# Two tiles' second-layer experts run in pairs behind the last dense pass, and the front stages get new spacings

## The reference

```python
h = W_E[tokens] * 16
h = h + time_and_channel_mix(layernorm(h))            # first layer's attention block
# first layer's experts ("dense"): 8 experts of 1024, mixed by a top-2 router, all computed
x = layernorm(h)
h = h + sum(w0[:, e] * (gelu(x @ W1[e] + b1[e]) @ W2[e] + b2[e]) for e in range(8))
# second layer's recurrence: k, v = x @ Wk, x @ Wr; running maximum, two scans, ratio
x = layernorm(h)
h = h + (sigmoid(r) * wkv(k, v)) @ Wo
# second layer's attention (16 heads of 16) and its four experts, top-2 of 4
x = layernorm(h)
xn = rms(x, n1_w); q, k, v = rms(heads(xn @ wq)), rms(heads(xn @ wk)), heads(xn @ wv)
x = x + zero_first_64(softmax(causal(q @ k.T)) @ v @ wo)
xf = rms(x, n2_w); w = top2(softmax(xf @ gate_w))
o0 = gelu(xf @ e0_up) @ e0_down
o1 = silu(xf @ e1_w1) * (xf @ e1_w2) @ e1_down
o2 = gelu(gelu(gelu(xf @ e2_l1) @ e2_l2) @ e2_l3) @ e2_l4
o3 = gelu(gelu(xf @ e3_down) @ e3_up) @ e3_out
h = h + x + zero_first_64(w[0]*o0 + w[1]*o1 + w[2]*o2 + w[3]*o3)
```

## Time and profile before

| | us |
|---|---|
| median of 3 runs | 3387.07 |
| profiled execution, its own time | 3385.92 |
| its span, first to last instruction | 3384.1 |
| PE busy (matmul) | 2812.2 |
| DVE busy | 1691.8 |
| ACT busy | 1785.9 |
| POOL busy | 1391.0 |
| granted TensorE clock, mean | 0.941 |

### The profile page before, as it was taken

One profiled execution on the slowest core, in us unless ns is written; L12 is line 12 of the kernel. 1 busy time (PEld: TensorE's weight loads), 2 busy tenths in 40 slices (PEclk: granted clock), 3 DMA queues, 4 the chain that ended last, 5 costly groups with the idle time before them and its releaser, 6 DMA issues. The chain is left out here.

```text
span 3384.1 us, 58992 instructions
## 1 busy us (share of the span) xinstructions
PE 2812.2 (83%) x21872; PEld 1878.7 (56%) x22208; DVE 1691.8 (50%) x3163; ACT 1785.9 (53%) x2817; POOL 1391.0 (41%) x1326
## 2 busy tenths in 40 slices
PE   3778776896888998899879987998799879985678
PEld 2445454564665666566646664666466646662455
DVE  6777745526346443644364436443544455445452
ACT  2535344555555565555555655565556555653433
POOL 5445433343344344434434443444334433442224
PEclk8999988999998999999999998999899989997889
DMA  1000007731121212222212121222121122211002
GB/s 64 13 19 19 12 13 269 269 119 50 63 80 57 77 68 71 72 82 76 79 56 83 68 87 56 83 68 74 68 83 68 68 72 79 74 51 38 27 27 64
DMA packets 62641, 242.58 MB, mean 72 GB/s; under 512 B 6784, under 2 KB 26528, under 8 KB 43552
## 3 DMA queue, kind: packets, MB, share of 16 engines
q1 hardware_dynamic: 60832, 234.69, 19.7%
q0 software_dynamic: 1536, 4.20, 0.4%
HBM read 207.13 MB, written 31.72 MB: 71 GB/s over the span
## 5 line engine op out<-in xcount | busy, mean ns | idle before, releaser
L1326 POOL TENSOR_TENSOR c_lo<-c_g,c_hi 128x512 bf16<-128x512 f32 x720 | 873.1, 1218 | 1580.1 <-ACT c_hi L1488 1407.7
L2151 PE MATMUL c_up<-c_xT,c_ring 128*128 128x512 bf16 x2877 | 720.5, 385 | 88.0 <-ACT c_hi L1488 31.7
L2168 PE MATMUL c_down<-c_ring,c_hi 128*128 128x256 bf16 x4096 | 718.0, 275 | 0.0
L1487 ACT ACTIVATE c_g<-c_up,b 128x512 f32<-128x512 f32 x512 | 353.3, 690 | 525.0 <-PE c_up L2151 492.9
L2168 PE MATMUL c_down<-c_ring,c_lo 128*128 128x256 bf16 x2048 | 564.4, 276 | 0.0
L2151 PEld LDWEIGHTS c_up<-c_xT,c_ring 128*128 128x128 bf16 x3072 | 294.0, 99 | 365.2 <-ACT c_hi L1488 39.6
L2168 PEld LDWEIGHTS c_down<-c_ring,c_hi 128*128 128x128 bf16 x4096 | 399.2, 99 | 113.1 <-issue 1.6
L1488 ACT ACTIVATE c_hi<-c_up,b 128x512 bf16<-128x512 f32 x512 | 350.7, 685 | 0.0
L1487 ACT ACTIVATE c_g<-c_up 128x512 f32<-128x512 f32 x176 | 106.2, 603 | 357.1 <-PE c_up L1917 356.7
L1754 DVE CAST c_room<-c_room 128x384 bf16<-128x384 f32 x256 | 146.0, 610 | 275.3 <-PE c_front L2063 260.9
L2168 PEld LDWEIGHTS c_down<-c_ring,c_lo 128*128 128x128 bf16 x2048 | 202.3, 99 | 25.3
(11 more groups left out here) (324 smaller groups left out, 5439.5 us busy)
## 6 DMA issues: line engine op xcount, KB each, us to landing
c_ring<-kept_dense SPq DMA_DIRECT2D x112, 1024.0 KB, 4.8
c_ring<-kept_experts SPq DMA_DIRECT2D x72, 512.0 KB, 3.3
c_room<-in_WB SPq DMA_DIRECT2D x16, 1024.0 KB, 7.4
kept_dense<-c_ring SPq DMA_DIRECT2D x16, 1024.0 KB, 4.9
c_ring<-kept_experts SPq DMA_DIRECT2D x32, 384.0 KB, 3.4
kept_experts<-c_room SPq DMA_DIRECT2D x9, 512.0 KB, 3.8
c_xT<-kept_xT SPq DMA_DIRECT2D x8, 512.0 KB, 4.1
out<-h SPq DMA_DIRECT2D x8, 512.0 KB, 4.4
```

The costliest lines, as they stand in the source:

```text
L1326: pool.tensor_tensor(lo14[:, a, :], g[:, h % 4, :], hi14[:, a, :], ALU.subtract).then_inc(lo_ready.sem, 1)
L1487: act.activation(g[:, h % 4, :], ub[n % 2][:, :], ACT.Gelu, bias=bias)
L2151: last = pe.matmul(ub[n % 2][:, :], r[:, wp, o + q * P:o + (q + 1) * P], xT[:, xp, q, :], start=(m == 0 and q == 0), stop=(m == 2 and q == ...
L2168: m = pe.matmul(bank, (hi14, lo14)[xp][:, a, s * P:(s + 1) * P], r[:, wp, o + KC * P:o + CHUNK], start=False, stop=(k == HC0 - 1 and n == ...
```

## The change

The loop ends one pass earlier (passes 3 to 6). Pass 7 holds dense work of tile 7 and the front of tile 6, and no experts. Pass 8 holds the front of tile 7 and the experts of tiles 5 and 6, expert by expert for the one and the other (`PAIR`), so that one load of weights serves two tiles; its planned work is 130.8 instead of 65.4. Pass 9 stays (tile 7). Tile 6's input of the experts goes into slots 0 and 1 of `hi14` and `lo14` (`y_parts`), its router weights into `wt_late` (`mixing`). The G units of a full pass stand ahead of D 41, 44, 47 and 50 instead of behind them, and the next U comes a D later (`ahead`). The numbers of `ORDER_F` change: their sum is 259.9; Rx0 and Rx1 get a number of their own, A1 stands behind Zx0 and ahead of Z0, and heads and maxima have new ones. In the list of a full pass D7 stands between Rb0 and Rc0 (before: behind Z0), with 11.7 of planned work from f0 to f1 (before 5.2) and 48.2 from f2 to f5 (before 40.4); in a pass without experts these are 7.8 (3.9) and 35.1 (29.9).

```diff
@@ heads_order, maxima_order, keys_order, ORDER_F
-        tokens += ["Sa%d" % n, "E%d" % n, "+1.3", "Sb%d" % n, "+2.6"]
+        tokens += ["Sa%d" % n, "E%d" % n, "+2.6", "Sb%d" % n, "+2.6"]
-        tokens += ["W%d" % n, "+3.9"]
+        tokens += ["W%d" % n, "+3"]
-    return " ".join("m%d +2" % (b * 6 + q) for q in range(6))
+    return " ".join("m%d +1.6" % (b * 6 + q) for q in range(6))
-    return ("Q%d +1.3 Qx%d +2 Q%d +1.3 Qx%d +2 X%d K%d +5 T%d +1.3 Tx%d K%d +5 T%d +1.3 Tx%d +1.5"
+    return ("Q%d +1.3 Qx%d +2.6 Q%d +1.3 Qx%d +2 X%d K%d +5 T%d +1.3 Tx%d K%d +5 T%d +1.3 Tx%d +1.5"
-    "f0 +3 r2x r2 +3 f1 +2.5 f1x +3 f2 +3 f2x A0 +7 Rx0 Ra0 +3 Rb0 +4 Rc0 A1 +6 Zx0 Z0 +5 Rx1 Ra1 +3 Rb1 +4 Rc1 +5 Zx1 Z1",
-    "+2 f5 +2 f5d +6 g5 +4 f6 +2 f6x +3", keys_order(0), maxima_order(0), "j0 +2 N0 +1 Nx0 +1.5", heads_order(0),
-    "+2 O0 +1", keys_order(1), maxima_order(1), "j1 +2 N1 +1 Nx1 +1.5", heads_order(1),
-    "+2 O1 +2 f13 +2 f13x +3 g13 +2 b0 +6 y0 +1 b1 +2 b1x +3 r1 +1.5")).split()
+    "f0 +5 r2x r2 +8 f1 +2.5 f1x +3 f2 +3 f2x A0 +8 Rx0 +3 Ra0 +3.5 Rb0 +6 Rc0 +5 Zx0 A1 +7 Z0 Rx1 +3 Ra1 +3.5 Rb1 +6 Rc1 +4 Zx1 Z1",
+    "+2 f5 +3 f5d +6 g5 +4 f6 +2 f6x +3.5", keys_order(0), maxima_order(0), "j0 +2 N0 +1 Nx0 +1.5", heads_order(0),
+    "+1.5 O0 +1", keys_order(1), maxima_order(1), "j1 +2 N1 +1 Nx1 +1.5", heads_order(1),
+    "+1.5 O1 +3 f13 +2 f13x +3 g13 +2 b0 +6 y0 +1 b1 +2 b1x +4 r1 +1.5")).split()
@@ make_plan
+PAIR = [("e2_l1", 0), ("e2_l1", 1), ("e2_l2", 0), ("e2_l2", 1), ("e2_l3", 0), ("e2_l3", 1), ("e0_up", 0), ("e2_l4", 0),
+        ("e0_up", 1), ("e2_l4", 1), ("e3_down", 0), ("e0_down", 0), ("e3_down", 1), ("e0_down", 1), ("e3_up", 0),
+        ("e3_up", 1), ("e1", 0), ("e3_out", 0), ("e1", 1), ("e3_out", 1), ("e1_down", 0), ("e1_down", 1)]
...
+        for u, d in zip(c_units("e1"), (41, 44, 47, 50)):
+            ahead[d] = u
     for d in range(NB):
-        while ups < min(d + LAG + 1, NB):
+        while ups < min(d + LAG + 1 - (d - 1 in ahead), NB):
...
+        if d in ahead:
+            plan.append(ahead[d])
         plan.append(("D", d))
@@ Plan (hidden slots of the passes without dense work)
-            self.home = {"e2_l1": 0, "e0_up": 8, "e2_l2": 4, "e2_l3": 0, "e3_down": 8, "e3_up": 4, "e1": 0}
+                self.home = {("e2_l1", 0): 2, ("e0_up", 0): 10, ("e2_l2", 0): 6, ("e2_l3", 0): 2, ("e3_down", 0): 10,
+                             ("e3_up", 0): 6, ("e1", 0): 2}
+                ups = [g for g in PAIR if g[0] not in DOWNS]
+                self.home = {g: 2 + 4 * (n % 3) for n, g in enumerate(ups)}
...
+PLAN_B, PLAN_BC, PLAN_CC, PLAN_C = Plan(True, 0), Plan(True, 1), Plan(False, 2), Plan(False, 1)
+LATE = TILES - 3
+def first_tile(i):
+    if isinstance(i, int):
+        return max(min(i - 2, LATE), 0) if i <= TILES else i - 2
+    return i - 2
@@ phase_bc
+        def y_parts(t):
+            return (hi14[:, 0:KC, :], lo14[:, 0:KC, :]) if isinstance(t, int) and t == TILES - 2 else (yhi, ylo)
+        def mixing(t):
+            return wt_late if isinstance(t, int) and t == TILES - 2 else wt
@@ run
-            with eng.Fori(3, TILES) as i:
+            with eng.Fori(3, TILES - 1) as i:
                 go(ORDER_BC, dense(i, PLAN_BC, PLAN_BC), front(i - 1), gates(i - 2))
-            go(ORDER_C, dense(TILES, PLAN_C, PLAN_BC), front(TILES - 1), gates(TILES - 2))
-            go(["r2x", "r2"] + PLAN_C.units, dense(TILES + 1, PLAN_C, PLAN_C), gates(TILES - 1))
+            go(ORDER_B, dense(TILES - 1, PLAN_B, PLAN_BC), front(TILES - 2), gates(LATE))
+            go(ORDER_CC, dense(TILES, PLAN_CC, PLAN_B), front(TILES - 1), gates(TILES - 2))
+            go(["r2x", "r2"] + PLAN_C.units, dense(TILES + 1, PLAN_C, PLAN_CC), gates(TILES - 1))
@@ sync, streamed
-                        sp.wait_ge(used_up.sem, used_up.at(i))
-                        keep(i - 3)
+                        for t in range(first_tile(i - 1), first_tile(i)) if isinstance(i, int) else (i - 3,):
+                            sp.wait_ge(used_up.sem, used_up.at(i))
+                            keep(t)
-            with sp.Fori(3, TILES) as i:
+            with sp.Fori(3, TILES - 1) as i:
                 streamed(i, PLAN_BC, PLAN_BC)
-            streamed(TILES, PLAN_C, PLAN_BC)
-            streamed(TILES + 1, PLAN_C, PLAN_C)
+            streamed(TILES - 1, PLAN_B, PLAN_BC)
+            streamed(TILES, PLAN_CC, PLAN_B)
+            streamed(TILES + 1, PLAN_C, PLAN_CC)
```

More of the change, by code:

```diff
@@ L803, with c_units @@
 NB, NG = E0 * HC0, 4
-def c_units(name):
+ONE = [(name, 0) for name in ("e2_l1", "e0_up", "e2_l2", "e0_down", "e3_down", "e2_l3", "e3_up", "e2_l4", "e1", "e3_out",
+                              "e1_down")]
+PAIR = [("e2_l1", 0), ("e2_l1", 1), ("e2_l2", 0), ("e2_l2", 1), ("e2_l3", 0), ("e2_l3", 1), ("e0_up", 0), ("e2_l4", 0),
+        ("e0_up", 1), ("e2_l4", 1), ("e3_down", 0), ("e0_down", 0), ("e3_down", 1), ("e0_down", 1), ("e3_up", 0),
+        ("e3_up", 1), ("e1", 0), ("e3_out", 0), ("e1", 1), ("e3_out", 1), ("e1_down", 0), ("e1_down", 1)]
+def c_units(name, j=0):
     if name == "e1":
-        return [("G", k) for k in range(HC)]
+        return [("G", k, j) for k in range(HC)]
     if name in DOWNS:
-        return [("O", name, k) for k in range(HC)]
-    return [("I", name, k) for k in range(UPS[name][2])]
+        return [("O", name, k, j) for k in range(HC)]
+    return [("I", name, k, j) for k in range(UPS[name][2])]
 def make_plan(dense, experts):
@@ L817, in make_plan @@
     if not dense:
-        for name in ("e2_l1", "e0_up", "e2_l2", "e0_down", "e3_down", "e2_l3", "e3_up", "e2_l4", "e1", "e3_out", "e1_down"):
-            plan += c_units(name)
+        for name, j in ONE if experts == 1 else PAIR:
+            plan += c_units(name, j)
         return plan
-    boundary, after = {}, {}
+    boundary, after, ahead = {}, {}, {}
     if experts:
@@ L855, in __init__ @@
         self.dense, self.experts = dense, experts
-        self.up, self.bank_user, self.hid, self.group = {}, [], {}, {}
+        self.up, self.bank_user, self.hid, self.group, self.gate = {}, [], {}, {}, {}
         n_hid = n_group = 0
@@ L864, in __init__ @@
                 self.bank_user += [u, u]
+                self.gate[u] = len(self.gate)
             if u[0] in "UIG":
@@ L871, in __init__ @@
             if u[0] == "O" and u[2] == 0:
-                self.group["c", u[1]] = n_group
+                self.group["c", u[1], u[3]] = n_group
                 n_group += 1
@@ L1018, in phase_bc @@
                   for j in range(2))
-        lg, pr, wt = (rest[:, 2 * SUB * E1 * E1 + j * SUB * E1:2 * SUB * E1 * E1 + (j + 1) * SUB * E1]
-                      .rearrange("p (s e) -> p s e", s=SUB) for j in range(3))
+        lg, pr, wt, wt_late, real = (rest[:, 2 * SUB * E1 * E1 + j * SUB * E1:2 * SUB * E1 * E1 + (j + 1) * SUB * E1]
+                                     .rearrange("p (s e) -> p s e", s=SUB) for j in range(5))
+        def mixing(t):
+            return wt_late if isinstance(t, int) and t == TILES - 2 else wt
         r1s = sb("r1", [P, 4, SUB])
@@ L1122, in phase_bc @@
             ORDER_0.append(u)
-        ORDER_B, ORDER_BC, ORDER_C = (plan.braid(ORDER_F) for plan in (PLAN_B, PLAN_BC, PLAN_C))
+        ORDER_B, ORDER_BC, ORDER_CC = (plan.braid(ORDER_F) for plan in (PLAN_B, PLAN_BC, PLAN_CC))
+        for order, last in ((ORDER_BC, ("G", HC - 1, 0)), (ORDER_CC, ("G", HC - 1, 0))):
+            assert order.index(last) < order.index("b1")
         def go(order, *stages):
@@ L1865, in step @@
                     elif u[0] == "O" and u[2] == HC - 1:
-                        e = DOWNS[u[1]][0]
-                        taken(plan.group["c", u[1]], i - 2, lambda s: wt[:, s, e:e + 1], ZERO)
+                        e, t = DOWNS[u[1]][0], first_tile(i) + u[3]
+                        taken(plan.group["c", u[1], u[3]], t, lambda s: mixing(t)[:, s, e:e + 1], ZERO)
                 return tokens_of(i, plan, step)
@@ L1871, in r2 @@
                 def r2():
-                    E.begin(t)
+                    wt = mixing(t)
+                    if not (isinstance(t, int) and t == TILES - 2):
+                        E.begin(t)
                     dve.wait_ge(lg_exp.sem, lg_exp.at(t))
@@ L2221, in expert_down @@
                             accumulator_free(group, s)
[L2222 removed]
+                        for n, (wp, xp) in enumerate(PARTS):
                             m = pe.matmul(ob[s // 2][:, (s % 2) * D:(s % 2) * D + DZ],
                                           (hi14, lo14)[xp][:, a, s * P:(s + 1) * P],
[L2225 to L2226 removed]
+                                          E(plan, wp, name, k, 0, DZ), start=(k == 0 and n == 0 and s % 2 == 0),
+                                          stop=(k == HC - 1 and n == 2), skip_group_check=True)
                         if k == HC - 1 and s % 2:
```

74 lines of the change are left out of this document (37 added, 37 removed).

## The result

The changed kernel takes 3429.7 us (median of 4 runs, 3428.3 to 3434.9), the kernel before 3387.2 on the same chip: a ratio of 1.013 (1.011 to 1.015). The prediction was 3282, its range 3250 to 3360. The profiled execution of the changed kernel spans 3428.2 us, 44.1 more than before, at a mean granted clock of 0.935 (before 0.941).

The account below looks back on a forecast made before the run. No engine bounds the whole: time is PE work plus idle time its written order leaves before tokens waiting for chains. Pass 7 -46 and -10, pass 8 +24, passes 2 to 6 -62, pass 1 -11: -105, giving 3282 us, range 3250 to 3360.

Parts of the forecast that it names:

- Pass 7: Tile 5's experts leave this pass, 46 us saved; the new spacing of its front saves 10 more.
- Pass 8: Tile 5's experts join: 65.4 us more PE work, mostly hidden in idle time, so +24, bounds 0 and +77.
- rival E: Pairs of tiles add eight pairs of ACT table loads that show in full, +21 us: 3303, chance 1 in 10.
- Pass 1: New spacing moves filler ahead of f1 and into the stretch from f2 to f5: 11 us saved.
- Gate units: In full passes, moved ahead of their D with the next U held back: net 2.5 us saved a pass.
- e0_down: In full passes, its 8.26 us accumulator wait falls to 3.7 with D7 ahead of Rc0; 1.2 appears at D8.
- f2 to f5: In full passes, grows from 58.1 to about 62 us with 7.8 more work in it: net 4 saved.
- Heads: In full passes, more filler between Sa and Sb covers second scores' waits for exponentials: net 4 us saved a pass.
- New stalls where filler went away: In full passes, stalls no profile row shows: cost 2.5 us a pass, bounds 0 and 12.
- The clock: In pass 8, PE at full clock for more of the pass gives back perhaps 2 us, from 0.81.
- Rival C: Passes 1 to 7: heads save nothing, filler ahead of f1 and f5 lengthens these; 6 us a pass, 3407, chance 0.08.
- Rival A: The spacing gives nothing, as a wait filled in one place opens in another: 3365, chance 0.16.

Follow-up runs that it names:

- mixed: The changed kernel with the old spacing numbers in full passes (2 to 6) and the new ones in passes 1, 7 and 8: 3341.3 us, 0.986.
- spacing_f0_f5: The kernel before with the new numbers of `ORDER_F` from f0 to Z1 alone: 3408.3 us, 1.007.
- spacing_only: The kernel before with the new numbers of `ORDER_F` alone: 3425.0 us, 1.012.
- pair_only: The changed kernel with the old `ORDER_F` and the gate units in their old places, leaving the pair of tiles: 3378.8 us, 0.998.
- gates_only: The kernel before with the gate units ahead of their D alone: 3371.9 us, 0.996.

## Why full passes got longer: an addition behind an accumulation

The stretch from f5 to Q0 is read on DVE (VectorE). Behind f5, DVE adds PE's product to `h` (f5d, L1666 before, L1708 after), then come statistics, a chain on POOL, the normalised input (L1517, L1559) and f6. The kernel before:

```profile
2120.44 0.69 DVE L1666 TENSOR_TENSOR h<-h,c_front 128x512 f32 x1 [2.01 <-PE c_front L1924]
2121.75 0.69 DVE L1666 TENSOR_TENSOR h<-h,c_front 128x512 f32 x1 [0.62 <-PE c_front L1924]
```

The changed kernel, DVE and then PE:

```profile
2168.60 1.66 DVE L1896 SCALAR_TENSOR_TENSOR h<-c_down,c_gates,h 128x256 f32 x4 [6.67 <-PE c_down L2211]
2170.17 1.28 DVE L1708 TENSOR_TENSOR h<-h,c_front 128x512 f32 x2
...
2177.02 3.86 DVE L1559 TENSOR_SCALAR c_xn<-h,c_fmv,c_frs 128x256 f32 x4 [3.59 <-POOL c_frs L1331]
```
```profile
2154.35 1.89 PE L1959 MATMUL c_up<-c_hi,c_ring 128*128 128x512 bf16 x8
...
2162.03 0.60 PE L1966 MATMUL c_front<-c_WF,c_xhi 128*128 128x256 bf16 x4 [2.33 <-ACT c_xhi L1435]
...
2180.93 1.97 PE L1973 MATMUL c_front<-ident,c_xn 128*128 128x128 f32 x8 [3.61 <-DVE c_xn L1559]
2182.69 3.62 PE L1959 MATMUL c_up<-c_hi,c_ring 128*128 128x512 bf16 x8
```

Before, the first addition starts 1.5 us after f5. Now DVE idles 6.7 us for the end of D15, accumulates it and adds 8.1 us after f5: the new list has f5, U18, D15, f5d, the old one f5, I e2_l2, f5d, U15, with D15 behind f6x. The work behind f5 no longer covers the chain, f6 waits 3.6 us, and the matmuls behind it run at half speed (eight in 3.62 us, the like ahead of f5 in 1.89). Of the 10.5 us that the stretch grew, 3.6 are this wait, some 2.2 a new one ahead of Q0, and 4.9 busy time at a clock of 0.83.

Two more accumulations stand differently in the new list. D39's comes behind X1, DVE's scaling and splitting of queries and keys, and e3_out waits 4.4 us for it. D47's comes behind G2, the gate unit, whose two operations on DVE wait for ACT; D48 waits 3.6 us for it. With the old numbers V4 and W5 stand between D47 and D48; with the new numbers and the gates in their old places D47 comes ahead of G2. In neither does D48 wait so. DVE in the changed kernel:

```profile
2308.39 1.38 DVE L1758 TENSOR_TENSOR c_ks<-c_room,c_ks 128x256 bf16<-128x256 f32 x1
2309.69 1.65 DVE L1896 SCALAR_TENSOR_TENSOR h<-c_down,c_gates,h 128x256 f32 x4
...
2359.20 0.69 DVE L1881 SCALAR_TENSOR_TENSOR c_sl<-c_sl,c_up 128x512 f32<-128x512 f32 x1 [10.08 <-ACT c_sl L1520]
2360.70 1.65 DVE L1896 SCALAR_TENSOR_TENSOR h<-c_down,c_gates,h 128x256 f32 x4
```

No run moves these two, so what they cost is not shown.

**after_f5d** puts f5d back ahead of U18 and D15 in the list of the full passes and moves nothing else:

```diff
+ORDER_FULL = " ".join(ORDER_F).replace("f5 +3 f5d +6 g5", "f5 +1 f5d +8 g5").split()
-   ... f5 U18 D15 f5d I(e2_l2, 3) U19 ...
+   ... f5 f5d U18 D15 I(e2_l2, 3) U19 ...
```

> The changed kernel with U18 and D15 behind f5d instead of ahead of it in the list of the full passes; no other token moves. If D15's accumulation ahead of f5d makes the chain to f6 late, the statistics end some 6 us earlier in each full pass, f6's wait of 3.6 us goes and f5 to Q0 shrinks from 30.1 to 22 to 26 us; with less half-clock time after it, full passes come to 348 to 352 and the total to 3385 to 3405. If the wait only opens again further on (PE idle stays at 42 us a pass), the total stays at 3420 to 3435.

3383.5 us, 1.000 (0.999 to 1.001), a little better than expected: f5d's one move takes off 46 us, as much as the changed kernel had lost in total. It is not all that the new numbers cost. Of the 88 us in full passes it gives back about half, and the loop's passes take 348 us where mixed takes 338 to 340. spacing_f0_f5 says the same from the other side: in its list f5d stands ahead of D15, and it is 23 us slower than the kernel before. Pass 5, from f5 to Q0, from there to its end, and the whole pass:

```profile
2137.30:2160.90 23.60, 21.25 (x130) 13.73 (x132) 10.83 (x24) 9.84 (x17) 12.27 (x16) 0.93 0.26 90
2160.90:2396.60 235.70, 207.99 (x1853) 146.42 (x1880) 92.26 (x201) 130.99 (x206) 93.51 (x86) 0.97 0.20 71
2048.40:2396.60 348.20, 307.28 (x2435) 205.97 (x2472) 157.93 (x302) 192.34 (x303) 145.02 (x133) 0.96 0.20 72
```

6.5 us are gone in the stretch itself and f6's wait with them; 4.0 more are gone behind Q0, where no token moved: the clock there is 0.97 instead of 0.95. So here the late chain cost its wait, and then the clock behind it. That is no rule: spacing_only has the same late D15 and the same wait of 3.6 us, and its loop pass shows 0.97.

**after_f5d_f6x** swaps a second pair of the kind, the unit I e2_l3 0, whose gelus stand on ACT between f6 and f6x:

```diff
-   ... f6 I(e2_l3, 0) f6x U21 D18 Q0
+   ... f6 f6x I(e2_l3, 0) U21 D18 Q0
```

> after_f5d with one more pair swapped in the list of the full passes: the unit I e2_l3 0 behind f6x instead of between f6 and f6x. If the wait ahead of Q0 is of the same kind as f6's was, f6 to Q0 shrinks from 8.5 to 5 to 6.5 us, full passes from 348 to 343 to 346 and the total to 3363 to 3375. If it is only moved on, the total stays at 3380 to 3387.

3381.2 us, 0.999 (0.998 to 1.000): a miss. f6 to Q0 shrinks from 8.7 to 6.1 us as expected and passes 2 and 3 by some 3 and 2, but the loop's passes 4 to 6 stay at 348, 348 and 345 us:

```profile
2047.70:2395.70 348.00, 311.98 (x2473) 208.04 (x2473) 158.38 (x302) 192.40 (x303) 144.81 (x133) 0.95 0.20 71
```

PE's waits in the pass add up to 35.5 us instead of 38.4, but the clock fell from 0.96 to 0.95, and the pass is as long as it was. How long a wait is doesn't tell what it costs.

## The clock and the loop

Two edits change no order. **after_fill** adds matmuls whose results nobody reads, 8 to 16 of 512 columns in each of five waits (f5, f6, Q0, the first O of e0_down and of e3_out; the first three also in passes 1, 7 and 8); they add work and leave nothing out. **after_unrolled** writes passes 3 to 6 out.

```diff
+            def keep_busy(bank, n):
+                for _ in range(n):
+                    pe.matmul(bank[:, :], c.identb[:, :], c.sel[:, 0:4, :], start=True, stop=True, ...)
...
+                    pe.wait_ge(tr_ready.sem, tr_ready.at(t))
+                    keep_busy(fb[2], 8)                        # ahead of f5
```
```diff
-            with eng.Fori(3, TILES - 1) as i:
+            for i in range(3, TILES - 1):
```

> The changed kernel, but TensorE multiplies two constant tiles into a free bank in five waits of each full pass (ahead of f5, f6, Q0, e0_down and e3_out; 8, 14, 8, 9 and 16 matmuls of 512 columns), whose results nobody reads: work is only added. Theory K (half-clock stretches behind short waits carry the loss in the loop's passes): the time at half clock in a loop pass falls from 44 us to 25 or less, and the pass gets shorter by 5 to 10 us though TensorE does more; total 3390 to 3415. Rival W (the waits carry it, the clock is only a witness): total 3428 or more.

> The changed kernel with its loop of passes 3 to 6 written out. Pass 2, written out, takes 342 us with 15 at half clock; passes 3 to 6, the same order in a loop, 355 to 359 with 39 to 44. If the loop itself (waits against registers, its turns) makes the difference, passes 3 to 6 take 340 to 345 and the total falls by 50 to 65 us. If it is where the waits fall in time that decides about the clock, the passes differ among themselves, somewhere from 340 to 358, total 3395 to 3430.

3377.8 us (0.997, 0.996 to 0.999) and 3373.5 (0.996, 0.994 to 0.997): they take 52 and 56 us off the changed kernel, the first more than expected. Pass 5 of the first and of the second:

```profile
2049.60:2394.20 344.60, 313.95 (x2527) 206.70 (x2527) 158.75 (x302) 192.34 (x303) 144.72 (x133) 0.99 0.21 72
```
```profile
2044.00:2385.70 341.70, 304.16 (x2475) 203.46 (x2473) 157.77 (x304) 192.59 (x303) 144.97 (x133) 0.98 0.21 72
```

With 55 matmuls more the pass is 14 us shorter, at 0.99 instead of 0.94. The edit lets nothing start earlier, so these 14 us can only come from matmuls that ran at the higher level. The Trainium skill (TensorE: Matmul & The Clock Gate, A second HAM failure mode: psum-queue depth-cycling) tells of a kernel whose frequent short idle times let the clock swing between its levels. These traces agree in part: pass 5 has 0.94 with eleven waits of 1.8 to 4.4 us, against 0.97 with six, two of them long. But the same order written out has ten waits of 1.8 to 4.3 us in its pass 5, the same ones but for the loop's, at 0.98. How many waits there are doesn't set the clock; where they fall matters, and what decides that stays open.

**after_shift** puts 8 such matmuls once between pass 2 and the loop, to learn whether the loop's slow pattern hangs on how it is entered.

> The changed kernel with 8 idle matmuls (1.7 us) once, between pass 2 and the loop; nothing in the loop differs. If the loop's passes fall into the same positions against the clock's decisions whatever they start from: passes 4 and 5 again 358 us with 44 at half clock, total 3425 to 3435. If the start decides: some other length, between 342 and 358, for all of them, total below 3420.

3434.2 us, 1.014 (1.012 to 1.016). Pass 2 is 8 us longer, and the loop's passes take 358.6, 358.3 and 358.5 us from f1 to f1 as without it. The loop falls into the same pattern from this start too.

**before_unrolled** and **before_fill** are the same edits in the kernel before (the second with 34 matmuls ahead of e0_down, 16 ahead of f1 in the loop and 6 in pass 2).

> The kernel before with its loop of four full passes written out. If the loop itself costs a full pass some us whatever the order (its loop passes took 341 us, and with the spacing mixed and gates ahead 338 in the loop and 334.5 written out), full passes come to 333 to 337 us and the total to 3360 to 3372. If only the changed kernel's pattern of waits locks into the loop's turns, the passes stay at 340 to 342 and the total at 3383 to 3390.

> The kernel before with idle matmuls of constants in its two long waits of a full pass (34 of 512 columns ahead of e0_down, whose wait is 8.3 us; 16 ahead of f1 in the loop, 6 in pass 2). Control for the filled version of the changed kernel. Theory K (the half-clock time behind waits costs half its length): a full pass has 17 to 24 us at half clock, the two long waits cause some 14 of it; total falls by 6 times 4 to 7 us, to 3345 to 3365. If the matmuls speed the kernel up in some other way, the gain isn't in the half-clock time; if waits alone count, 3385 to 3395.

Written out: 3363.2 us, 0.994 (0.993 to 0.996). The loop has five turns here, not the four of the expectation. In the profiled execution, the fastest of the four (3355.4 us), all full passes take 334.5 us; start to f2 takes 18.5 instead of 24, and from f2 on they take 316 and 317. So there a turn of the loop costs the kernel before 6 us, at the place where DVE idles 5.4; by the medians it is 22 us over five turns, 4 each. The Trainium skill (Runtime: NRT & Kernel Launch, Instruction fetch mechanics) says that a taken branch out of the prefetched window stalls the engine, and that kernels therefore unroll; these runs agree, in that DVE's idle time at the turn is gone, though nothing in them shows a fetch of instructions. With matmuls: 3383.6, 0.999 (0.998 to 1.000), a miss (3345 to 3365 was expected). Pass 2 gained 5 us, the loop's passes none, though their clock rose from 0.97 to 0.98; f2 comes at 24 as before. The trace of pass 5 shows where the gain went. Behind the filled wait of e0_down the clock is 1.00 instead of 0.96, and the stretch to the next wait takes 43.4 us instead of 44.9. Behind U48's wait of 2.8 us, which is the same in both, it is the other way round, 1.7 us lost; first the kernel before, then this one:

```profile
2297.20:2307.10 9.90, 8.80 (x68) 6.13 (x68) 3.87 (x8) 7.50 (x11) 7.12 (x7) 1.00 0.08 12
2298.80:2310.40 11.60, 10.55 (x70) 6.73 (x69) 3.85 (x8) 7.52 (x11) 7.16 (x7) 0.85 0.05 8
```

The same wait is followed by a clock of 1.00 in one run and of 0.85 in the other.

**after_unrolled_fill** and **after_f5d_fill** take loop and clock away together, without and with the swap of D15.

> The changed kernel with its loop written out and the added matmuls in the same five waits. If the new order costs the full passes by half-clock time and by the loop alone, they come down from 341 to 346 (written out) and 345 (with the matmuls in the loop) to 329 to 333, level with the mixed kernel's, and the total to 3305 to 3325. If the many short waits cost by themselves (PE idle 37 us a pass against 31 of the mixed kernel written out), they stop at 336 to 341 and the total at 3340 to 3360.

> The same swap in the changed kernel with its loop written out and added matmuls in the waits, where neither loop nor half-clock time is left to speak of (full passes 340 us). If the swap is worth its wait alone, f5 to Q0 shrinks from 25.8 to 21 to 22 us (it keeps 14 added matmuls, about 3 us, in front of f6), full passes come to 336 and the total to 3340 to 3350; if it is worth nothing by itself, the passes stay at 340 and the total at 3360 to 3366.

3363.2 us (0.994, 0.993 to 0.996) and 3353.8 (0.990, 0.988 to 0.992). The first is above both of its expectations' totals, with full passes inside the second's; the other lies between its two. They take 340 us in the first kernel and 338 in the other; pass 5 of the first:

```profile
2033.40:2373.60 340.20, 314.44 (x2528) 207.12 (x2527) 157.39 (x301) 192.59 (x303) 144.94 (x133) 0.99 0.21 73
```

The swap is worth 2 us a pass where the loop is written out and the waits are filled, 10 in the loop without either.

**mixed_fill**, **mixed_unrolled** and **mixed_unrolled_fill** do the same to mixed (matmuls ahead of e0_down and f1 in full passes, and in five waits of passes 1, 7 and 8).

> The mixed version (old spacing in full passes, new one elsewhere) with idle matmuls in its waits: as in the filled kernel before for full passes, and in passes 1, 7 and 8 ahead of D8, f5, f6, T0 and T2, each shorter than the wait. Theory K: half-clock time of full passes from 17 to 24 down to 10 or less, of pass 8 from 51 to 30; total 3295 to 3320. If waits alone count: 3341 or more.

> The mixed version with passes 3 to 6 written out. The turns of the loop cost DVE 5.4 us of idle time each, of which PE shows 5 to 6 as a longer wait ahead of f1: three turns and their half-clock stretches, 15 to 25 us less: 3315 to 3328. If that wait is covered anyway: 3335 to 3345.

> The mixed kernel (new spacing in passes 1, 7 and 8, old in the full ones) with loop written out and the added matmuls. The matmuls alone gave 29 us, writing out alone 10. If the two gains add, full passes come to 329 to 331 and the total to 3296 to 3306; if both only remove the same half-clock time, the passes stay at 333 to 335 and the total at 3308 to 3316.

3312.6 us (0.977, 0.976 to 0.979), 3331.7 (0.983, 0.982 to 0.985; a little above the expected 3315 to 3328) and 3287.3 (0.972, 0.971 to 0.974; below the expected 3296 to 3306). The last is the fastest kernel of all, 98 us under the kernel before on its chip; the two gains over mixed, 29 and 10, come to 54 together. Its pass 5:

```profile
1992.90:2320.90 328.00, 305.16 (x2515) 204.45 (x2513) 159.51 (x303) 193.16 (x303) 144.45 (x133) 1.00 0.22 76
```

328.0 against 340.2 with the new numbers, both written out and filled: the new spacing costs a full pass 12 us even so. Of these 3.2 are the 15 more added matmuls (six of 512 columns take 1.29 us at full clock), 2.7 are PE's waits (25.1 against 22.4), and the clock, 0.99 against 1.00, is most of the rest.

## Why the prediction was wrong, step by step

- **Pass 7**: -46 and -10 were predicted, -43.5 (pair_only) and -9.4 (from 295.7 to 286.3) measured; 286.3 lies in the forecast's 280 to 290. Right.
- **Pass 8**: +24 predicted, +30.6 measured, inside 265 to 285, at a clock of 0.91 against 0.81. Right in kind, 7 us short in size. By pair_only it would be +37 without the new spacing; which of the small terms was short isn't shown. It wasn't rival E: the trace has 19 table loads in pass 8 where it had 17, one pair more and not eight.
- **Pass 1**: -11 predicted, -4.9 measured; half the size.
- **Gate units**: 2.5 a pass predicted, 2.3 measured (gates_only).
- **e0_down** waits 2.5 us where 3.7 was predicted, D8 not at all where 1.2 was; U48's wait is gone, but D48 (L2208) has one of 3.6. **f2 to f5** is 63.5 us where about 62 was predicted. Up to here the step was sound.
- **Heads**: the exponentials' waits fell from 5.1 us to 0.8, as forecast with a net of 4. But Q0 to the pass's end is no shorter (239.7 against 239.5), since e3_out and D48 now wait and the clock is lower.
- **"New stalls where filler went away"**, 2.5 us with 12 as the upper bound: this is the step that failed. The full passes missed by 134 us (+72 against -62), 27 a pass, and a bound of 12 didn't hold it. It looked for stalls only in the heads, took the clock of these passes for unchanged, and took the size of a wait from how much filler surrounds it. One stall came between f5 and Q0, where filler stayed the same and f5d came to stand behind D15; undoing it gave 46 us. Two more, 4.4 and 3.6 us, came at e3_out and D48 in the same way. The prediction had placed D7's accumulation among DVE's tokens for the new list, but not D15's, D39's or D47's. That accounts for about half of the 88 us by which the new full passes are behind mixed's; the other half lies in those two waits and the clock and is not taken apart by a run.
- **The clock** was priced in pass 8 alone. In the full passes it fell from 0.97 to 0.94 and took some 12 of pass 5's 18 us; after_fill gave 14 back.
- **The loop** was known from the earlier trace rows, but only as a shift of the pass's start. That a slow pattern can repeat itself in each turn (358 us in the loop, 341 to 345 written out) was in no step.
- **Sums.** The stages of pass 8 add up to 17, not 18; 65.4 plus four times 2.7 is 76, not 77; five times 12 is 60, not 62. Put right, the forecast is 3283, as far off as before.

Rival C, 0.08, was the nearest: slower, in full passes, by filler put ahead of f5; at its 6 us a pass it gave 3407, and measured are 14. Its mechanism (the heads save nothing and f1 and f5 get longer) is only half of it: start to f5 grew by 7.3 us, the stretch behind it by 10.5. Rival A's "a wait filled in one place opens in another" is what the list of waits shows. Both were weighed at 0.24 together against a sum whose largest term, -62, rested on waits taken away one at a time.

## What to carry to other kernels

When numbers of a written-out order change, list for every in-order engine which tokens swapped places, and look above all for a chain's operation that came to stand behind one that waits for another engine; one such swap cost 46 us here and no sum of fillers shows it. A wait removed is a gain only if PE's clock and the next wait agree: price a full pass at both levels of the clock. And two parts of a change that each have a price alone may have another together, as gates and spacing had. Where waits can't be removed, matmuls with unread results inside them and a loop written out brought, with the parts of the change that held, 3287 us against 3385.
